# A four-stage token tower on one Trainium2 core: second-half attention operands on GpSimd and ScalarE, a norm split in two, routed input on 64-row tiles

## The chip, the cores and the metric

The kernel runs on one core of one Trainium2 chip, in one launch for the whole problem. The metric is the time of an execution on the device in microseconds (us). Three executions before the change gave a median of 1512.79 us (1504.69 to 1515.6). A further execution was profiled; its trace is the source of all rows.

## The reference, cut to what matters

```python
h = tok(x)                                        # masked scores, values, PReLU
h = layernorm(h + mamba(h))                       # 16-state scan
h = layernorm(h + experts(h))                     # 16 experts, top 2
h = layernorm(h + window_attention(h))            # this stage and its norm are touched
h = layernorm(h + routed_ffn(h))                  # its first matmul is touched

def window_attention(x):                          # windows of 64 tokens, 8 heads of 8
    q, k, v = split_heads(x @ w_qkv.T)            # x: 8 x 1024 x 64, float32
    a = q @ k.T * 8 ** -0.5 + rel_bias[rel_idx]
    return (softmax(a) @ v) @ w_proj.T + b_proj

def routed_ffn(x):
    h = relu(x @ Wi.T + bi)                       # 64 -> 128
    for l in range(2):
        h = relu(h @ (Ws[l] + Wr[l, route] + I).T + bs[l] + br[l, route])
    return h @ Wo.T + bo
```

## The kernel before

The eight sequences are worked on in four pairs, one after the other. A pair puts the 64 features of one sequence on partitions 0 to 63 and those of the other on 64 to 127; 1024 tokens lie along the free dimension, in two halves of 512 (`NC = 2`). All engines run written-out programs, and the order on each engine is the order in which the Python code emits its instructions; they meet at semaphores whose counts per pair stand in `PER`. There is no scheduler.

The attention runs in `NM = 8` steps of two windows. The operands come first: for each half, `att_inputs(c)` on TensorE makes keys, queries and values in PSUM (L687, L688, L691); ScalarE copies the keys (L985), scales the first head's block into `kb` (L987) and copies the queries (L990). `kb` holds the keys four times, each masked to one head. The other three heads are scaled by VectorE in `k_blocks(c)` (L1259). The values go to `vb`, four copies for each half: the first half on ScalarE (L999), the second on VectorE (L1283).

A step m then goes through: scores on TensorE (L735, `att_scores`), bias added and row maxima taken on VectorE (L1268, L1272, `bias_max`), maxima subtracted on GpSimd (L462, the shift), exponential on ScalarE (L1008), eight transposes on TensorE (L748, `att_turn`), their copy on ScalarE (L1014), products with the values on TensorE (L762, `att_values`), reciprocal and scaling on VectorE (L1296, L1301, `att_norm`), a transpose of the output (L768) with its copy on ScalarE (L1020), and the projection (L775), which adds to the residual in PSUM banks 6 and 7. TensorE's loop emits in turn s the scores of step s, the transposes of s-2, the value products of s-3, the output transpose of s-4 and the projection of s-5. Steps 0 to 3 belong to the first half, 4 to 7 to the second. In turn 1 it also puts the residual into banks 6 and 7 (L788).

A norm works on four chunks of 256 tokens (`NN = 4`): squares on ScalarE (L862), variance by a matmul with an averaging matrix (L486), Ln and Exp on ScalarE (L868, L873), product on VectorE (L1064 here, L1067 in the norm before). The norm of the attention, number 2, comes when all eight projections are done: ScalarE waits for `proj_ps` of all. Then the routed stage starts with `f_in`, L804: for each half, two matmuls over all 128 partitions with a weight `fiT` whose other half is zero, so that each picks one sequence; the routed layers follow at L814. The row maxima of step m must have been shifted before step m+2 overwrites the biased scores, and the shift's buffer is freed by the exponential two steps earlier.

## Time and profile before

| | before |
|---|---|
| median of three runs | 1512.79 us |
| these runs | 1504.69 to 1515.6 us |
| the profiled execution | 1513.76 us |
| its span, first to last instruction | 1512.0 us |
| TensorE matmul, VectorE, ScalarE, GpSimd busy | 85%, 68%, 39%, 30% |
| mean granted TensorE clock | 0.943 |

Times in the rows are microseconds from the first instruction unless marked ns. PE is TensorE's matmul, PEld its weight load, DVE is VectorE, ACT ScalarE, POOL GpSimd; L862 is line 862 of the kernel before. A granted clock of 1.00 is 2.4 GHz, 0.50 is 1.2 GHz. One float32 matmul of the program appears as two instructions in the trace. The third pair, whose attention runs from 1071 to 1117 us, is used for single rows.

### The profile page before, as it was taken

Reading aid. Unit: us, or ns where it says so; the run is one execution under the profiler, and the core shown is the slowest. Engines: PE = TensorE matmul, PEld = TensorE weight load, DVE = VectorE, ACT = ScalarE, POOL = GpSimd, SP = SyncE. Lnnn points to the kernel's source line nnn. Section 1 sums busy time; section 2 is a strip of 40 time slices with the busy share of each in tenths; the row PEclk is TensorE's granted clock in tenths of the full one; section 3 lists DMA queues with packets and bytes.
Section 4 is the critical chain, followed back from the end, with each engine's and each line's share of the span. In section 5 each row is a group of like instructions: output and inputs, shape, how many; then the busy total and the mean of one; then the engine's idle time right before and its main releaser. Section 6 shows DMA issues by size and latency. Waiting matters only on the chain. (4 is left out here: it accounts for less than half of the span.)

```text
span 1512.0 us, 16650 instructions
## 1 busy us (share of the span) xinstructions
PE 1292.1 (85%) x5930; PEld 562.1 (37%) x5930; DVE 1031.3 (68%) x1130; ACT 592.0 (39%) x815; POOL 455.7 (30%) x230
## 2 busy tenths in 40 slices
PE   6957789989995778998998677999899677899988
PEld 2222333348532223333742223333473232333366
DVE  3599965664449996567555999556756599865683
ACT  0354343333425344332525443532451634343245
POOL 3268800022005881001200788000210189600030
PEclk9979999997897999999999799999999889999998
DMA  8334420000003342000001344200000134220000
GB/s 245 104 129 155 146 69 12 1 1 1 15 0 129 143 143 83 22 1 1 2 15 44 113 149 143 69 2 1 1 1 15 59 125 167 98 57 0 1 2 15
DMA packets 43379, 93.66 MB, mean 62 GB/s; under 512 B 6786, under 2 KB 23970, under 8 KB 42786
## 3 DMA queue, kind: packets, MB, share of 16 engines
q1 hardware_dynamic: 42690, 88.25, 17.5%
q10 hardware_dynamic: 608, 4.34, 1.0%
q8 instruction: 49, 0.80, 0.2%
q14 instruction: 32, 0.26, 0.1%
HBM read 87.84 MB, written 4.73 MB: 61 GB/s over the span
## 5 line engine op out<-in xcount | busy, mean ns | idle before, releaser
L448 POOL TENSOR_TENSOR scratch<-scratch 128x1024 f32<-128x1024 f32 x124 | 297.4, 2413 | 354.7 <-DVE scratch L1152 353.1
L598 PE MATMUL ps<-scratch,consts 128*128 128x512 f32 x512 | 257.8, 638 | 6.2 <-POOL scratch L448 6.2
L462 POOL TENSOR_TENSOR scratch<-scratch,rmax 128x1024 f32<-128x1024 f32 x32 | 61.6, 1925 | 598.3 <-DVE rmax L1272 598.3
L1152 DVE TENSOR_TENSOR_SCAN scratch<-ps,scratch 128x1024 f32<-128x1024 f32 x100 | 225.5, 2278 | 0.5
L925 ACT ACTIVATE ps<-steps,vec 128x1024 f32<-128x1024 f32 x128 | 142.9, 1117 | 207.1 <-DVE scratch L1152 205.2
L1201 DVE TENSOR_TENSOR scratch<-scratch,ps 128x1024 f32<-128x1024 f32 x108 | 131.8, 1221 | 128.6 <-PE ps L659 117.7
L576 PE MATMUL ps<-bc,pick 128*128 128x512 bf16 x256 | 84.7, 416 | 139.0 <-DVE scratch L1141 101.7
L971 ACT ACTIVATE scratch<-ps 128x1024 f32<-128x1024 f32 x108 | 108.9, 1023 | 175.5 <-PE ps L646 175.5
L598 PEld LDWEIGHTS ps<-scratch,consts 128*128 128x128 f32 x512 | 104.8, 207 | 127.2 <-issue 100.5
L646 PE MATMUL ps<-h_odd,w 64*128 64x512 f32 x512 | 140.9, 636 | 3.8 <-ACT scratch L971 3.8
L1141 DVE TENSOR_TENSOR scratch<-steps,ps 128x1024 f32<-128x1024 f32 x100 | 122.0, 1220 | 28.8 <-PE ps L576 23.5
L659 PE MATMUL ps<-scratch,w 64*128 64x512 f32 x512 | 134.9, 602 | 7.2 <-DVE scratch L1201 7.2
L667 PE MATMUL ps<-scratch,to_model 128*64 128x512 f32 x512 | 138.1, 618 | 1.4 <-DVE scratch L1201 1.4
L1101 DVE TENSOR_TENSOR scratch<-ps,decayT 128x1024 f32<-128x1024 f32 x64 | 77.0, 1222 | 38.3 <-PE ps L515 26.5
L576 PEld LDWEIGHTS ps<-bc,pick 128*128 128x128 bf16 x256 | 19.0, 98 | 224.3 <-issue 218.0
L1208 DVE TENSOR_TENSOR scratch<-h_odd,ps 128x512 f32<-128x512 f32 x128 | 87.6, 687 | 19.3 <-PE ps L678 19.3
L456 POOL TENSOR_TENSOR work<-steps,work 128x1024 f32<-128x1024 f32 x28 | 66.1, 2360 | 33.2 <-ACT work L935 32.9
L659 PEld LDWEIGHTS ps<-scratch,w 64*128 64x128 f32 x512 | 47.3, 186 | 73.2 <-issue 70.7
L529 PE MATMUL ps<-scratch,xc 128*64 128x512 f32 x256 | 67.3, 614 | 4.5 <-DVE scratch L1101 4.5
L646 PEld LDWEIGHTS ps<-h_odd,w 64*128 64x128 f32 x512 | 39.7, 184 | 83.1 <-issue 83.1
L515 PE MATMUL ps<-steps 64*128 64x512 f32 x256 | 70.1, 634 | 0.0
L762 PE MATMUL ps<-vb,zs 128*128 128x36 f32 x512 | 65.6, 288 | 0.3
(197 smaller groups left out, 1610.0 us busy)
## 6 DMA issues: line engine op xcount, KB each, us to landing
scratch<-c_rows SPq DMA_DIRECT2D x128, 512.0 KB, 3.7
steps<-routed_table SPq DMA_DIRECT2D x128, 64.5 KB, 1.9
decayT<-in_decayT SPq DMA_DIRECT2D x8, 512.0 KB, 15.6
work<-in_table ACTq DMA_DIRECT2D x1, 2064.0 KB, 13.2
routed_table<-work SPq DMA_DIRECT2D x1, 2064.0 KB, 6.3
w<-in_w ACTq DMA_DIRECT2D x4, 512.0 KB, 20.8
out<-h_even SPq DMA_DIRECT2D x4, 512.0 KB, 2.6
bc<-in_x_next SPq DMA_DIRECT2D x3, 512.0 KB, 3.6
```

The costliest lines, as they stand in the source:

```text
L448: pool.tensor_tensor(hc_slot(k), hs_slot(k), c_slot(k), ALU.mult).then_inc(sem["hc_ready"], 1)
L576: m = mm(ps[:, c, :], pick[:, n:n + 1].to_broadcast([P, P]), bc[:, g, c * CH:(c + 1) * CH], start=True, stop=True)
L598: m = mm(ps[:, 6 + c, :], ident, hc_slot(k)[:, c * CH:(c + 1) * CH], start=(n == 0), stop=(n == NS - 1))
L646: m = mm(ps[:, first_bank(j) + g, :], w12[half, 0, e, :], h[1][half, c * CH:(c + 1) * CH], start=True, stop=True)
L659: m = mm(ps[:, 2 + g, :], w12[half, 1, e, :], x_gated(j)[half], start=True, stop=True)
L667: m = mm(ps[D * g:D * g + D, 4 + c, :], w3[:, e, :], hidden_slot(j)[:, g, :], start=False, stop=True, skip_group_check=True)
L925: act.activation(banks(dA_bank(k)), dt[:, k // NS, :], ACT.Exp, scale=v("A", k % NS))\
L971: act.activation(silu_slot(j), ps[:, first_bank(j):first_bank(j) + 2, :], ACT.Silu).then_inc(sem["silu_ready"], 1)
L1141: dve.tensor_tensor(dbu_slot(k), u[:, k // NS, :], banks(0), ALU.mult)\
L1152: dve.tensor_tensor_scan(hs_slot(k), banks(dA_bank(k)), dbu_slot(k), 0.0, ALU.mult, ALU.add).then_inc(sem["scanned"], 1)
L1201: dve.tensor_tensor(hidden_slot(j), silu_slot(j), ps[:, 2:4, :], ALU.mult).then_inc(sem["hidden"], 1)
L1208: dve.tensor_tensor(x_gated(j), h[1][:, c * CH:(c + 1) * CH], ps[:, 6 + j % 2, :], ALU.mult).then_inc(sem["x_gated"], 1)
```

## The change

Four edits, all in the attention and what follows it.

- The second half's three key blocks move from VectorE to GpSimd, behind the shift of step 1, with a semaphore of their own, `k_blocks_pool`, on which TensorE waits before the scores of the second half.
- The second half's four value copies move from VectorE to ScalarE, behind its `att_inputs(1)`.
- Chunks 0 and 1 of the attention's norm no longer wait for all projections. Their squares stand on ScalarE in turn 8, their variance matmuls on TensorE at the end of turn 9, their Ln and Exp on ScalarE in turn 9, ahead of the last copy of a transposed output. Chunks 2 and 3 follow the last projection; on TensorE their variance matmuls stand behind the first half's `f_in`. Their PSUM banks change.
- `f_in` uses the two 64-row halves of TensorE: `fiT` holds the weight once on each half, and each matmul reads 64 partitions. One memset at the start is dropped.

```diff
+                    if m == 1:
+                        pool.wait_ge(sem["k_copied"], at(pair, "k_copied", NC))
+                        for hh in range(K_SPLIT, HQ):
+                            pool.tensor_scalar(kb[:, WIN[1], hh, :],
+                                               k_sb[:, TOK[1]].rearrange("p (a b) -> p a b", b=WS),
+                                               head_mask[:, hh:hh + 1], None, ALU.mult)\
+                                .then_inc(sem["k_blocks_pool"], 1)
...
-        VAR_BANKS = ((2, 3, 4, 5), (0, 1, 6, 7), (0, 1, 2, 3), (6, 7, 2, 3))
+        VAR_BANKS = ((2, 3, 4, 5), (0, 1, 6, 7), (0, 1, 4, 5), (6, 7, 2, 3))
...
-                    pe.wait_ge(sem["k_blocks_dve"], at(pair, "k_blocks_dve", (HQ - K_SPLIT) * (c + 1)))
+                    pe.wait_ge(sem["k_blocks_dve"], at(pair, "k_blocks_dve", HQ - K_SPLIT))
+                    if c:
+                        pe.wait_ge(sem["k_blocks_pool"], at(pair, "k_blocks_pool", HQ - K_SPLIT))
...
                         att_proj(s - 5)
-                norm(2)
+                    if s == NM + 1:
+                        pe.wait_ge(sem["biased"], at(pair, "biased", NM))
+                        norm(2, range(NN // NC))
                 for c in range(NC):
                     pe.wait_ge(sem["h_ready"], at(pair, "h_ready", 2 * NN + NN // NC * (c + 1)))
                     for g in range(2):
-                        mm(ps[:, 2 * g + c, :], fiT[:, g, :], h[3][:, c * CH:(c + 1) * CH],
+                        half = slice(D * g, D * g + D)
+                        mm(ps[:, 2 * g + c, :], fiT[half, :], h[3][half, c * CH:(c + 1) * CH],
                            start=True, stop=True).then_inc(sem["f_in_ps"], 1)
+                    if c == 0:
+                        norm(2, range(NN // NC, NN))
...
                 att_inputs(1)
+                v_blocks(1)
                 for s in range(NM + 4):
...
+                    if s == NM:
+                        squares(2, range(NN // NC))
+                    if s == NM + 1:
+                        roots(2, range(NN // NC))
-                norm(2)
+                norm(2, range(NN // NC, NN))
...
                 bias_max(0)
-                k_blocks(1)
-                dve.wait_ge(sem["av_ps"], at(pair, "av_ps", NC))
-                av = ps[:, 5, :].rearrange("p (w g hp d) -> p w g hp d", w=NW // NC, g=2, hp=H // 2)
-                for a in range(2):
-                    half = slice(D * a, D * a + D)
-                    for g in range(2):
-                        dve.tensor_copy(vb[half, WIN[1], :, g, a, 0:HD], av[half, :, g, :, :])\
-                           .then_inc(sem["v_blocks_dve"], 1)
...
-            pool.memset(projT, 0.0)
-            pool.memset(fiT[:, :, :], 0.0).then_inc(zeroed, 1)
+            pool.memset(projT, 0.0).then_inc(zeroed, 1)
```

`norm` on ScalarE is now `squares` followed by `roots`, and `v_blocks(c)` is the old copy loop for either half. Line numbers shift: L1268, L1272 and L1296 become L1296, L1300 and L1316; L1008, L1014 and L1020 become L1032, L1038 and L1044; L486, L748, L762, L768, L775, L804, L814 become L493, L757, L770, L776, L783, L815, L827; L862, L868, L873 become L876, L885, L890.

VectorE at the start of the attention, before the change, from the maxima of step 0 to those of step 2:

```order
L1272 TENSOR_REDUCE rmax<-scratch 128x16 [waits biased]
L1259 TENSOR_SCALAR scratch<-scratch,consts 128x8x64 [waits k_copied]
L1259 TENSOR_SCALAR scratch<-scratch,consts 128x8x64 x2
L1283 COPY vb<-ps 64x32x8 [waits av_ps]
L1283 COPY vb<-ps 64x32x8 x3
L1268 TENSOR_TENSOR scratch<-ps,rows 128x1024 [waits att_ps]
L1272 TENSOR_REDUCE rmax<-scratch 128x16 [waits biased]
L1268 TENSOR_TENSOR scratch<-ps,rows 128x1024 [waits shifted,att_ps]
L1272 TENSOR_REDUCE rmax<-scratch 128x16 [waits biased]
```

The same place after it:

```order
L1300 TENSOR_REDUCE rmax<-scratch 128x16 [waits biased]
L1296 TENSOR_TENSOR scratch<-ps,rows 128x1024 [waits att_ps]
L1300 TENSOR_REDUCE rmax<-scratch 128x16 [waits biased]
L1296 TENSOR_TENSOR scratch<-ps,rows 128x1024 [waits shifted,att_ps]
L1300 TENSOR_REDUCE rmax<-scratch 128x16 [waits biased]
```

The three scalings (of `scratch`, where `kb` lies) and the four copies are gone; the bias of step 1 follows the maxima of step 0 directly.

TensorE at the end of the attention, before the change, from the output transpose of step 6 to the routed input:

```order
L762 MATMUL ps<-vb,zs 128x2x18 x7
L768 MATMUL ps<-consts,scratch 128x128 [waits normed]
L775 MATMUL ps<-scratch,to_model 64x64 [waits outT_sb]
L775 MATMUL ps<-scratch,to_model 64x64 x3
L768 MATMUL ps<-consts,scratch 128x128 [waits normed]
L775 MATMUL ps<-scratch,to_model 64x64 [waits outT_sb]
L775 MATMUL ps<-scratch,to_model 64x64 x3
L775 MATMUL ps<-scratch,to_model 64x64 [waits outT_sb]
L775 MATMUL ps<-scratch,to_model 64x64 x3
L486 MATMUL ps<-work,consts 128x256 [waits squared] x4
L804 MATMUL ps<-h_odd,fiT 128x512 [waits h_ready]
L804 MATMUL ps<-h_odd,fiT 128x512
```

After it, two places of the same program, the early variance matmuls and the end:

```order
L783 MATMUL ps<-scratch,to_model 64x64 x3
L493 MATMUL ps<-work,consts 128x256 [waits squared,biased]
L493 MATMUL ps<-work,consts 128x256 [waits squared]
L770 MATMUL ps<-vb,zs 128x2x18 [waits outT_sb,v_blocks,probT_sb]
L770 MATMUL ps<-vb,zs 128x2x18 x7
L776 MATMUL ps<-consts,scratch 128x128 [waits normed]
```

```order
L783 MATMUL ps<-scratch,to_model 64x64 x3
L815 MATMUL ps<-h_odd,fiT 128x512 [waits h_ready]
L815 MATMUL ps<-h_odd,fiT 128x512
L493 MATMUL ps<-work,consts 128x256 [waits squared] x2
L815 MATMUL ps<-h_odd,fiT 128x512 [waits h_ready]
L815 MATMUL ps<-h_odd,fiT 128x512
```

Two variance matmuls now stand ahead of the value products of step 7, the other two between the halves of the routed input.

ScalarE at the same end, after the change:

```order
L1038 ACTIVATE zs<-ps 128x1024 [waits pv_ps,probT_ps]
L1044 ACTIVATE scratch<-ps 128x128 [waits proj_ps,outT_ps]
L876 ACTIVATE work<-ps,out_bias 128x256 [waits proj_ps] x2
L1044 ACTIVATE scratch<-ps 128x128 [waits proj_ps,outT_ps]
L885 ACTIVATE work<-ps,vec 128x256 [waits var_ps] x2
L890 ACTIVATE work<-work 128x256 [waits act_chain] x2
L1044 ACTIVATE scratch<-ps 128x128 [waits proj_ps,outT_ps]
L876 ACTIVATE work<-ps,out_bias 128x256 [waits proj_ps] x2
```

Two squares stand between the output copies (L1044) of steps 5 and 6, two Ln and two Exp between those of steps 6 and 7; before, three such copies followed each other and all four squares came after them.

## Rows read from the trace of the kernel before

**Rows 1.** Busy time by window, attention to routed layers, first and third pair.
```profile
core 0: us, PE busy (x) PEld busy (x) DVE busy (x) ACT busy (x) POOL busy (x), PEclk, DMA share, GB/s
320.21:387.99 67.78, 60.99 (x449) 45.56 (x449) 35.78 (x62) 27.20 (x45) 15.39 (x8) 0.75 0.00 1
...
1070.89:1125.44 54.55, 47.87 (x449) 36.05 (x449) 35.78 (x62) 26.86 (x45) 15.40 (x8) 0.94 0.00 1
```

**Rows 2.** Timeline, third pair: start, length, engine, line, idle before and releaser.
```profile
1073.73 1.22 DVE L1272 TENSOR_REDUCE rmax<-scratch 128x16 f32<-128x1024 f32 x1
...
1074.86 2.92 DVE L1259 TENSOR_SCALAR scratch<-scratch,consts 128x512 f32<-128x512 f32 x3
...
1076.63 1.99 PE L788 MATMUL ps<-h_even,consts 128*128 128x512 f32 x4
...
1077.13 1.06 ACT L1008 ACTIVATE xc<-scratch 128x1024 f32<-128x1024 f32 x1 [1.69 <-POOL scratch L462]
...
1077.70 1.54 DVE L1283 COPY vb<-ps 64x256 f32<-64x256 f32 x4
1079.27 1.23 DVE L1268 TENSOR_TENSOR scratch<-ps,rows 128x1024 f32<-128x1024 f32 x1
...
1080.64 1.09 PE L735 MATMUL ps<-scratch 32*64 32x256 f32 x16 [2.02 <-DVE scratch L1268]
...
1081.83 1.90 POOL L462 TENSOR_TENSOR scratch<-scratch,rmax 128x1024 f32<-128x1024 f32 x1 [4.73 <-DVE rmax L1272]
...
1085.88 1.06 PE L748 MATMUL ps<-consts,xc 128*128 128x128 f32 x8 [1.62 <-ACT zs L1014]
...
1087.25 1.00 ACT L1014 ACTIVATE zs<-ps 128x1024 f32<-128x1024 f32 x1
...
1089.60 1.09 PE L748 MATMUL ps<-consts,xc 128*128 128x128 f32 x8
```

**Rows 3.** Busy time by window, third pair's middle steps and its end.
```profile
1090.00:1108.00 18.00, 18.00 (x196) 15.78 (x194) 14.02 (x24) 9.37 (x13) 7.61 (x4) 1.00 0.00 1
1114.00:1120.00 6.00, 5.06 (x34) 3.77 (x34) 1.09 (x4) 2.90 (x8) 0.00 (x0) 0.50 0.00 1
```

**Rows 4.** Timeline, third pair, from the last value products to the routed layers.
```profile
1112.16 2.06 PE L762 MATMUL ps<-vb,zs 128*128 128x36 f32 x16
...
1115.88 1.13 PE L775 MATMUL ps<-scratch,to_model 128*64 128x64 f32 x16
...
1117.06 1.57 ACT L862 ACTIVATE work<-ps,out_bias 128x256 f32<-128x256 f32 x4 [0.79 <-PE ps L775]
...
1117.59 3.51 PE L486 MATMUL ps<-work,consts 128*128 128x256 f32 x8 [0.57 <-ACT work L862]
...
1121.90 3.70 PE L804 MATMUL ps<-h_odd,fiT 128*128 128x512 f32 x8 [0.81 <-DVE h_odd L1064]
...
1125.44 7.31 PE L814 MATMUL ps<-scratch,steps 128*128 128x128 f32 x64
```

**Rows 5.** GpSimd's groups of instructions: busy us, mean ns | idle before.
```profile
L399 POOL MEMSET vb<- 128x2304 f32 x1 | 2.0, 2023 | 0.0
...
L415 POOL TENSOR_TENSOR in_x<-in_x,scratch 128x512 f32<-128x512 f32 x1 | 1.3, 1272 | 12.7 <-DMA route<-in_route 12.7
```

**Rows 6.** Timeline, third pair: half of the norm ahead of the attention.
```profile
1069.39 0.66 ACT L862 ACTIVATE work<-ps 128x256 f32<-128x256 f32 x2 [4.73 <-PE ps L667]
...
1069.83 1.13 PE L486 MATMUL ps<-work,consts 128*128 128x256 f32 x4 [0.48 <-ACT work L862]
1070.56 0.91 ACT L868 ACTIVATE work<-ps,vec 128x256 f32<-128x256 f32 x2 [0.51 <-PE ps L486]
...
1071.37 0.71 ACT L873 ACTIVATE work<-work 128x256 f32<-128x256 f32 x2
1071.81 0.76 DVE L1067 TENSOR_TENSOR h_even<-ps,work 128x256 f32<-128x256 f32 x2 [2.41 <-ACT work L873]
```

**Rows 7.** Chain of waits, expert stage: start us, us, what.
```profile
1343.16 1.06 PE ps L646 x4
```

More of the change, by code:

```diff
@@ L81 @@
     aq_ps=NC, ak_ps=NC, av_ps=NC, k_copied=NC, q_scaled=NC, k_blocks=NC * K_SPLIT,
-    k_blocks_dve=NC * (HQ - K_SPLIT), v_blocks=4, v_blocks_dve=4, att_ps=NM, biased=NM, row_max=NM, shifted=NM, att_exp=NM,
+    k_blocks_dve=HQ - K_SPLIT, k_blocks_pool=HQ - K_SPLIT, v_blocks=4 * NC, att_ps=NM, biased=NM, row_max=NM, shifted=NM, att_exp=NM,
     probT_ps=NM, probT_sb=NM, pv_ps=NM, normed=NW, outT_ps=NM, outT_sb=NM, proj_ps=NM,
@@ L144, in build_tower @@
         av_bd = sb("av_bd", [P, P])
-        fiT = sb("fiT", [P, 2, HID])
+        fiT = sb("fiT", [P, HID])
         c_dram = nc.dram_tensor("c_rows", (2, NS, T), F32, kind="Internal").ap()
@@ L342, in _ @@
                 (pick[:, :], i["pick"]), (out_wT, i["out_wT"]), (w3, i["w3"]),
-                (foT, i["foT"]), (fiT[0:D, 0, :], i["fiT"]), (fiT[D:P, 1, :], i["fiT"]),
+                (foT, i["foT"]), (fiT[0:D, :], i["fiT"]), (fiT[D:P, :], i["fiT"]),
                 (gate_bd[0:D, 0:NX], i["gate_w"]), (gate_bd[D:P, NX:2 * NX], i["gate_w"]),
@@ L753, in att_values @@
                     pe.wait_ge(sem["probT_sb"], at(pair, "probT_sb", m_ + 1))
-                    pe.wait_ge(sem["v_blocks"], at(pair, "v_blocks", 4))
-                    pe.wait_ge(sem["v_blocks_dve"], at(pair, "v_blocks_dve", 4))
+                    pe.wait_ge(sem["v_blocks"], at(pair, "v_blocks", 4 * NC if m_ else 4))
                     if m_ >= 2:
@@ L851, in then, with squares, roots @@
                     link(act, act_chain, per, pair, count, ins)
-                def norm(k, chunks=range(NN)):
+                def squares(k, chunks):
                     for c in chunks:
+                        part = c // (NN // NC)
                         if k == 1:
-                            act.wait_ge(sem["expert_ps"], at(pair, "expert_ps", NX * (c // (NN // NC) + 1)))
+                            act.wait_ge(sem["expert_ps"], at(pair, "expert_ps", NX * (part + 1)))
                         elif k == 2:
-                            act.wait_ge(sem["proj_ps"], at(pair, "proj_ps", NM))
+                            act.wait_ge(sem["proj_ps"], at(pair, "proj_ps", NM // NC * (part + 1)))
                         else:
-                            act.wait_ge(sem["r_ready"], at(pair, "r_ready", R_COUNT[k] + c // (NN // NC) + 1))
+                            act.wait_ge(sem["r_ready"], at(pair, "r_ready", R_COUNT[k] + part + 1))
                         act.activation(sq[:, c * NCH:(c + 1) * NCH], res_chunk(k, c), ACT.Square,
                                        bias=res_bias(k) if k >= 2 else 0.0).then_inc(sem["squared"], 1)
+                def roots(k, chunks):
                     before = count[0]
@@ L874, in norm @@
                     count[0] += len(chunks)
+                def norm(k, chunks=range(NN)):
+                    squares(k, chunks)
+                    roots(k, chunks)
                 for c in range(NC):
@@ L991, in att_inputs, with v_blocks @@
                        .then_inc(sem["q_scaled"], 1)
-                att_inputs(0)
-                act.wait_ge(sem["av_ps"], at(pair, "av_ps", 1))
-                av = ps[:, 4, :].rearrange("p (w g hp d) -> p w g hp d", w=NW // NC, g=2, hp=H // 2)
-                for a in range(2):
-                    half = slice(D * a, D * a + D)
-                    for g in range(2):
-                        act.activation(vb[half, WIN[0], :, g, a, 0:HD], av[half, :, g, :, :], ACT.Copy)\
-                           .then_inc(sem["v_blocks"], 1)
+                def v_blocks(c):
+                    act.wait_ge(sem["av_ps"], at(pair, "av_ps", c + 1))
+                    av = ps[:, 4 + c, :].rearrange("p (w g hp d) -> p w g hp d", w=NW // NC, g=2, hp=H // 2)
+                    for a in range(2):
+                        half = slice(D * a, D * a + D)
+                        for g in range(2):
+                            act.activation(vb[half, WIN[c], :, g, a, 0:HD], av[half, :, g, :, :], ACT.Copy)\
+                               .then_inc(sem["v_blocks"], 1)
+                att_inputs(0)
+                v_blocks(0)
                 norm(1, range(NN // NC, NN))
                 att_inputs(1)
+                v_blocks(1)
                 for s in range(NM + 4):
@@ L1276, in _ @@
                 bias_max(0)
-                k_blocks(1)
-                dve.wait_ge(sem["av_ps"], at(pair, "av_ps", NC))
-                av = ps[:, 5, :].rearrange("p (w g hp d) -> p w g hp d", w=NW // NC, g=2, hp=H // 2)
-                for a in range(2):
-                    half = slice(D * a, D * a + D)
-                    for g in range(2):
-                        dve.tensor_copy(vb[half, WIN[1], :, g, a, 0:HD], av[half, :, g, :, :])\
-                           .then_inc(sem["v_blocks_dve"], 1)
                 def att_norm(m_):
```

## The prediction

> **What bounds the kernel now.** I read the page's busy shares first: TensorE carries 85% of the span, VectorE 68%, but the shares mix stages with different limits, so the edited stretch has to be read by itself. The table of windows gives it for two of the four pairs, from the first scores of the attention to the first routed matmul [rows 1]. In the third pair it takes 54.55 us with TensorE busy for 47.87, in the first 67.78 us, with the same instructions at a mean granted clock of 0.75 instead of 0.94. All four together are 231 us of the 1512, and everything outside them is left as it was but for one memset.
>
> The timeline of the third pair then tells what ends last in it. Read [rows 2] from the top: VectorE finishes the row maxima of step 0, spends 2.92 us on the key blocks of the second half and 1.54 us on its value blocks, and only then adds the bias of step 1, at 1079.27. Its scores had been there since 1076.63, when TensorE went on to the next line. TensorE waits 2.02 us for that addition, and 1.62 us more two steps later. From 1090 to 1108 it is busy for 18.00 of 18.00 us [rows 3]: there TensorE alone sets the pace, and what is won before is carried along. Behind the last projection comes a serial chain at the clock's lower level (1114 to 1120: 0.50, so 1.2 GHz) [rows 3, 4]: four squares, four variance matmuls, four Ln and Exp, four products, then the routed input, 8.4 us from the first square at 1117.06 to the first routed matmul at 1125.44 [rows 4].
>
> **The head.** All arithmetic is for the third pair. Without the 2.92 and 1.54 us the bias of step 1 can start when its scores are there, 1076.75 with a hop, instead of 1079.27. But TensorE still has the four matmuls that end at 1078.62 in front of the scores of step 2, which began at 1080.64: the head can give at most 2.0 us [rows 2].
>
> The three key blocks now stand on GpSimd between the shift of step 1 and that of step 2. Queued behind them are the shifts; ScalarE's exponential waits for the shift, its copy of the transposed probabilities stands behind the exponential, and TensorE's next transposes wait for that copy. The bias takes 1.23 and the maxima 1.22, so shift 1 runs from 1079.3 to 1081.25; with a price p for a block, shift 2 ends at 1083.15 + 3p, the exponential (1.06) and the copy (1.00) at 1085.2 + 3p, and the transposes of step 2 start at 1085.35 + 3p where they started at 1089.60 [rows 2]. So the head gives 4.25 - 3p, no more than 2.0.
>
> No row shows p. Below stands the rate of the GpSimd memset of 2304 columns, 2.02 us, which is 0.45 us for 512 columns with nothing read; above, the 512-column GpSimd product of two tensors, 1.27 us [rows 5]. The nearest row is the shift itself: one full tensor, 16 repeated values, 1.90 us for 1024 columns, so 0.95 for 512 [rows 2]. A block reads one tensor and a single column, a little less: I take **p = 0.9, gain 4.25 - 2.7 = 1.55 us** (2.0 at the lower end, 0.43 at the upper).
> The Trainium skill (GPSIMD Engine Reference, sections 3.1 and 4.1) calls GpSimd the wrong engine for ordinary elementwise work, yet nearly line rate with one input; its best measured case for 512 elements, 0.77 us, taken as an estimate of p, would make the head 1.94. Its warning speaks against the move, and the 1.55 to 1.94 us between the two values of the head's arithmetic show how little turns on it.
> At p = 0.9 the blocks are ready at 1083.95. The scores of step 4, their first reader, stand on TensorE behind the transposes of step 1 (at 1085.88 before, at 1083.9 at the earliest now [rows 2]) and the value products of step 0, so they find them ready.
>
> The value blocks on ScalarE cost nothing: four copies took VectorE 1.54 us, and ScalarE sits idle 1.69 us in front of the exponential of step 0 [rows 2]. Without that cover the exponential would end 1.5 us later, at 1079.7; its transposes stand behind scores that start at 1078.6 at the earliest and take 1.1, so even that would be hidden.
>
> **The tail.** Three things move. First, half of the norm leaves the chain. At full clock a half norm, two squares to the end of two products, took 1069.39 to 1072.57, 3.2 us [rows 6]. Behind the last projection there now run: this half (3.3 with the longer form of its last operation), with the first half's routed input between squares and matmuls. On two row tiles of 64 that input costs what a pair of 64-row matmuls costs in the expert stage, 1.06 us [rows 7], against 3.54 / 2 = 1.77 for half of the old form [rows 4]. It begins with the squares while the variance matmuls could have begun 0.44 later, so it adds 0.6; the second half's input adds 1.06. Sum 3.3 + 0.6 + 1.06 = 5.0 instead of 8.4: 3.4 us won. ScalarE and VectorE read these results as before.
>
> Second, the early half stands in front of other work. On TensorE two variance matmuls (1.13 us [rows 6]) and a wait for the squares, some 0.3, stand ahead of the value products of step 7: 1.4 us. What is queued behind: these products, the last reciprocals, the last transposes, the last projections, so the whole end of the chain. On ScalarE the two Ln and two Exp (0.91 + 0.71 less a little overlap, 1.5 us [rows 6]) stand ahead of the last copy of the output's transpose; between the copies of steps 6 and 7 there is most of that room, and I let 0.3 stick out (0 to 1.5). So 3.4 - 1.7 = 1.7 us at the clock of before.
>
> Third, the clock. The old stretch ran at 0.50; its eight variance instructions took 3.51 us, four at full clock 1.13 [rows 4, 6]. With the new matmuls in between the clock may stay up, which is worth 0.5 more (2.2), or fall later, over both halves of the routed input and the last variances: 2 x 1.06 + 0.6 lost, -1.0. I take **1.2 us**, since the stretch is still thin on TensorE.
>
> **The sum.** (1.55 + 1.2) x 4 = 11.0. The smaller memset of the routed weight frees the loads behind it 0.3 us sooner, once; the loads are the same in number. 1513.76 (span and start-up of the profiled execution) - 11.3 = 1502.5. The median of the runs shown is 1.0 below that execution, so the forecast for a median is **1501.5 us**. Both ends of both prices give 4 x (0.43 - 1.0) = -2.3 to 4 x (2.0 + 2.2) = 16.8 us, 1515 to 1496.
>
> **The rivals.**
> *The first pair loses its slow stretch.* It took 13.2 us more than the third with the same instructions, all of it at the lower clock [rows 1]. What went before was thin work on TensorE, with waits like the 2.02 and 1.62 us of [rows 2], and the change takes the first of them away. Against it: the three other pairs have the same waits and kept their clock, so a small shift decides. 1501.5 - 13.2 = 1488.
>
> *One more pair falls into it.* Each pair now starts its attention at another moment than before, and the wait of the second transposes for the copy stays. 1501.5 + 13.2 = 1515.
>
> *The change moves the wait only.* Blocks at 1.27 us hold the shifts, and the early norm half costs TensorE what it saves: (0.43 + 0) x 4 = 1.7, 1511. For it speaks that TensorE runs without a gap from 1090 on [rows 3], so that 1.4 us put into its order there are paid in full.
>
> *Slower.* The place is the same, the transposes of step 1 with TensorE waiting; the price is 13.2 us a pair; it decides from the second additional pair on: 1501.5 + 26.4 = 1528, with a third 1541. Against it: only one pair of four showed it.
>
> **How the numbers follow.** Forecast, 1496 to 1507: 0.42. First pair clean, about 1488: 0.22. One more slow pair, about 1515: 0.15. Wait only moved, 1507 to 1515: 0.13. Two more slow pairs: 0.08. The range 1488 to 1517 leaves out half of the clean case and the last one, some 0.2. The line between faster and same is 1% of 1512.79, so 1497.7, and 1527.9 on the other side, about what a measurement of this kernel can tell from no change. Faster: the clean case and the best of the forecast, 0.22 + 0.09 = 0.31; slower 0.08; same 0.61. The likeliest outcome by itself is thus a small gain of 0.7% (1496 to 1507).
>
> **What the profile of the changed kernel would show.** VectorE's bias of step 1 starts about 1.8 us after the maxima of step 0 end, where it was 4.3. Three GpSimd scalings of 0.9 us between the second and third shift. TensorE's wait of 2.02 us gone, the second transposes' wait still there. Two variance matmuls ahead of the last value products, four instructions of 64 rows in about 1.06 us for each half of the routed input, and some 5 us from the last projection to the first routed matmul. The stretch in pairs two to four at about 51.8 us instead of 54.5. I am wrong if a scaling takes over 1.4 us, if the stretch's mean clock falls below 0.9 in more than one pair, or if the roots hold the last copy by more than 1 us.

## The result and the profile after

The changed kernel takes 1534.03 us in the median of four runs (1531.84 to 1538.66), the kernel before 1514.19 beside it. The ratio is **1.0123 [1.0067, 1.0179]**: slower by 1.2%, where 1501.5 with a range of 1488 to 1517 was forecast. A second group of runs on another occasion gave 1533.77 and 1.0105 [1.0027, 1.0182]. The kernel before spreads from 1502 to 1533 us by itself, of which more below. Ratios compare fast executions alone and so leave out those of a kernel that are over 1.5% above its fastest; beside the experiments these were 13 of 25, 8 of 19 and 4 of 13 executions of the kernel before, and its medians with them are 1527, 1523 and 1516 us.

The windows of the changed kernel, from the first scores to the first routed matmul of the four pairs (columns: window, its length, busy time and count of TensorE, its weight loads, VectorE, ScalarE, GpSimd, then the granted clock, the DMA share and GB/s):

```profile
325.23:385.40 60.17, 52.05 (x450) 39.73 (x449) 31.33 (x55) 27.30 (x48) 19.77 (x11) 0.86 0.00 1
700.50:760.66 60.16, 52.04 (x449) 39.72 (x448) 31.33 (x55) 27.31 (x48) 19.77 (x11) 0.86 0.00 1
1076.31:1136.46 60.15, 52.03 (x450) 39.71 (x449) 31.33 (x55) 27.30 (x48) 19.77 (x11) 0.86 0.01 1
1451.56:1511.71 60.15, 52.03 (x449) 39.71 (x448) 31.33 (x55) 27.41 (x48) 19.77 (x11) 0.86 0.00 1
1094.00:1111.00 17.00, 15.71 (x92) 12.94 (x93) 6.62 (x13) 6.59 (x9) 4.81 (x3) 0.54 0.01 2
```

All four pairs are alike, at 60.15 us with a clock of 0.86. Before, the third took 54.55 and the first 67.78 [rows 1]. So three pairs lost 5.5 to 5.7 us each and the first won 7.6. Of the 18.0 us between the two spans (1512.0 and 1530.0) the pairs two to four hold 16.8, the first -7.6, its later beginning 5.0 (325.23 against 320.21, where the second profile of the kernel before starts at 326.39, so this does not go with the change), and the rest, between and behind the stretches, 3.8.

The timeline of the third pair shows where the 5.6 come from (start, length, engine, line, what, and in brackets the idle time ahead of it):

```profile
1082.19 1.22 DVE L1296 TENSOR_TENSOR scratch<-ps,rows 128x1024 f32<-128x1024 f32 x1 [1.82 <-PE ps L744]
...
1083.97 1.09 PE L744 MATMUL ps<-scratch 32*64 32x256 f32 x16
...
1084.75 1.90 POOL L461 TENSOR_TENSOR scratch<-scratch,rmax 128x1024 f32<-128x1024 f32 x1 [2.40 <-DVE rmax L1300]
...
1086.63 4.65 POOL L470 TENSOR_SCALAR scratch<-scratch,consts 128x512 f32<-128x512 f32 x3
...
1091.24 3.76 POOL L461 TENSOR_TENSOR scratch<-scratch,rmax 128x1024 f32<-128x1024 f32 x2
1091.64 1.09 PE L744 MATMUL ps<-scratch 32*64 32x256 f32 x16
...
1093.18 1.06 ACT L1032 ACTIVATE xc<-scratch 128x1024 f32<-128x1024 f32 x1 [4.39 <-POOL scratch L461]
...
1094.14 1.01 ACT L1038 ACTIVATE zs<-ps 128x1024 f32<-128x1024 f32 x1
...
1095.29 1.94 PE L757 MATMUL ps<-consts,xc 128*128 128x128 f32 x8 [2.56 <-ACT zs L1038]
...
1097.02 3.25 PE L770 MATMUL ps<-vb,zs 128*128 128x36 f32 x15
```

VectorE is free at once, as intended: the bias of step 1 comes 1.82 us after the maxima of step 0 and the scores of step 2 no longer wait. But three GpSimd blocks take 4.65 us, and behind them stand shift 2, its exponential, the copy, and TensorE, idle for 2.56 us ahead of the transposes of step 2. From there its clock is 0.50: eight transposes take 1.94 us instead of 1.09, and the low stretch lasts 17 us in every pair (the last row of the windows is the third's). The end of the stretch:

```profile
1130.50 0.94 PE L783 MATMUL ps<-scratch,to_model 128*64 128x64 f32 x16
...
1131.43 1.13 PE L815 MATMUL ps<-h_odd,fiT 64*128 64x512 f32 x4
...
1132.49 1.13 PE L493 MATMUL ps<-work,consts 128*128 128x256 f32 x4
...
1134.47 0.88 DVE L1092 SCALAR_TENSOR_TENSOR h_odd<-ps,out_bias,work 128x256 f32<-128x256 f32 x2 [3.09 <-ACT work L890]
...
1135.40 1.13 PE L815 MATMUL ps<-h_odd,fiT 64*128 64x512 f32 x4 [1.78 <-DVE h_odd L1092]
...
1136.46 7.41 PE L827 MATMUL ps<-scratch,steps 128*128 128x128 f32 x64
```

From the end of the last projections, 1131.44, to the first routed matmul it takes 5.02 us, at full clock, where it took 8.43 [rows 4] with a clock of 0.50 up to about 1120.7 and of 1.00 behind that. So the tail does what it was to do, and the loss lies between the transposes of step 2 and the last projections. In a table, in us, with two experiments from below:

| third pair | first scores to transposes of step 2 | to the end of the last projections | to the first routed matmul | sum |
|---|---|---|---|---|
| before | 18.71 | 27.41 | 8.43 | 54.55 |
| changed | 18.98 | 36.15 | 5.02 | 60.15 |
| changed, TensorE kept busy (e6) | 20.03 | 28.15 | 5.01 | 53.19 |
| changed, blocks on ScalarE (e4) | 16.35 | 28.21 | 5.02 | 49.58 |

### The profile page after: what moved, and what is told of

Read it like the earlier page. It is cut to its first block and busy times, and to the rows that moved or that the text cites. A ratio compares the mean times of both kernels' runs of the same rounds, so it can differ in the third digit from the quotient of the medians.

```text
span 1530.0 us, 16613 instructions
## 1 busy us (share of the span) xinstructions
PE 1294.0 (85%) x5914; PEld 568.2 (37%) x5930; DVE 1019.2 (67%) x1102; ACT 596.5 (39%) x831; POOL 474.2 (31%) x241
## 5 line engine op out<-in xcount | busy, mean ns | idle before, releaser
L605 PE MATMUL ps<-scratch,consts 128*128 128x512 f32 x512 | 254.7, 631 | 6.3 <-POOL scratch L447 6.3
L770 PEld LDWEIGHTS ps<-vb,zs 128*128 128x128 f32 x512 | 74.5, 230 | 0.2
L770 PE MATMUL ps<-vb,zs 128*128 128x36 f32 x512 | 73.3, 307 | 0.0
```

Source lines behind the costliest of these rows:

```text
L605: m = mm(ps[:, 6 + c, :], ident, hc_slot(k)[:, c * CH:(c + 1) * CH], start=(n == 0), stop=(n == NS - 1))
L770: last = mm(o[:, :, hp, :], att_probT(m_)[:, b * P:(b + 1) * P], vb[:, 2 * m_ + ww, hp].rearrange("p g a b -> p g (a b)"), start=True, sto ...
```

## The experiments

The theory: GpSimd's blocks hold shift 2, TensorE idles, its clock falls for 17 us, and this costs 8 us a pair. The rivals: the new tail costs the time; the low clock is chance; the late shift costs by itself, whatever the clock. Times are medians of up to ten executions; pairs are read from the one that was profiled, which for e1, e2, e4, e5, e6 and e9 took 5 to 13 us less than the median. What the longer executions held is not shown.

**One edit undone, and each half of the change alone.** e1 puts the three key blocks back on VectorE:

```diff
-                    if m == 1:
-                        pool.wait_ge(sem["k_copied"], at(pair, "k_copied", NC))
-                        for hh in range(K_SPLIT, HQ):
-                            pool.tensor_scalar(kb[:, WIN[1], hh, :],
...
                 bias_max(0)
+                k_blocks(1)
...
```

> The changed kernel with one edit undone: the three key blocks of the second half stand on VectorE again, behind the row maxima of step 0; the values on ScalarE and the early norm half stay. Theory (the GpSimd blocks of 1.57 us hold the shift of step 2, TensorE waits 2.56 us for its transposes, and its clock falls to 0.50 for 17 us in every pair): the 2.56 us wait and the 0.50 stretch at the transposes of step 2 are gone in at least three pairs, the stretch from first scores to first routed matmul is 50 to 52 us there instead of 60.15, and the time is 1495 to 1508. Rival (the early norm half, or chance, brings the low clock): the low stretches stay in three or four pairs, 1525 to 1540.

Measured: 1523.7 us, ratio to the kernel before 1.0071 [1.0009, 1.0133]; the profiled execution took 1510.78. The time missed the expectation by 16 us. Of the mechanism, half came: the wait ahead of the transposes of step 2 is gone in all four pairs, but only two took 50.49 us at full clock, where at least three were expected; the others took 60.04 and 53.54.

```profile
325.77:376.26 50.49, 44.08 (x449) 33.29 (x448) 34.07 (x58) 27.31 (x48) 15.39 (x8) 1.00 0.00 1
691.95:751.99 60.04, 53.62 (x450) 40.74 (x449) 34.07 (x58) 27.41 (x48) 15.39 (x8) 0.83 0.00 1
```

Here TensorE waits 1.76 us ahead of the transposes of step 1 in every pair (VectorE's 2.92 us of blocks are late there), and with that wait one pair of four fell to 0.50 for 20.5 us, another for 3.4. So with the GpSimd blocks every pair falls, and without them fewer do, but they are not the only way to it.

e2 is the head of the change alone, on the kernel before (the same blocks on GpSimd, the same values on ScalarE, nothing of the norm):

```diff
+                    if m == 1:
+                        pool.wait_ge(sem["k_copied"], at(pair, "k_copied", NC))
+                        for hh in range(K_SPLIT, HQ):
+                            pool.tensor_scalar(kb[:, WIN[1], hh, :],
...
-                k_blocks(1)
...
+                v_blocks(1)
...
```

> The kernel before with the head of the change alone: key blocks of the second half on GpSimd behind the shift of step 1, their values on ScalarE; norm and routed input as before. Theory: the wait of about 2.56 us ahead of the transposes of step 2 and 17 us of 0.50 clock in all four pairs, the stretch about 62.8 us in each (60.15 and the 2.6 that the tail gave), so some 8 us more in three pairs and 5 less in the first: 1530 to 1545. Rival (the tail costs the time, the head is worth about nothing): 1510 to 1516, clock stretches as in the kernel before.

Measured: 1548.21 us, 3 above the interval, 1.0263 [1.0172, 1.0353]. Three pairs took 64.75 to 64.84 us at 0.79, the last 57.88. The first and the last:

```profile
323.25:388.00 64.75, 57.70 (x449) 42.84 (x449) 31.51 (x55) 28.44 (x49) 19.77 (x11) 0.79 0.00 1
1462.18:1520.06 57.88, 50.84 (x449) 38.13 (x449) 31.51 (x55) 28.55 (x49) 19.77 (x11) 0.88 0.01 1
```

TensorE waits 2.56 us ahead of the transposes of step 2 in all four, and the clock falls behind it in all four, in the last for only 7 us. The head alone costs more than the whole change, so the tail is not the cause.

e3 is the tail alone, on the kernel before (early norm half, 64-row routed input):

```diff
+                    if s == NM + 1:
+                        pe.wait_ge(sem["biased"], at(pair, "biased", NM))
+                        norm(2, range(NN // NC))
...
-                        mm(ps[:, 2 * g + c, :], fiT[:, g, :], h[3][:, c * CH:(c + 1) * CH],
+                        half = slice(D * g, D * g + D)
+                        mm(ps[:, 2 * g + c, :], fiT[half, :], h[3][half, c * CH:(c + 1) * CH],
...
```

> The kernel before with the tail of the change alone: norm's first half inside the last steps and the routed input on 64-row tiles; key and value blocks as before. Theory: the tail gives 2.6 us a pair and leaves the clock in the head as it was: 1499 to 1506, stretch 52 us in pairs with the full clock. Rival (the tail's new order brings the low clock or costs as much as it saves): 1513 or more.

Measured: 1515.9 us, 1.0026 [0.9981, 1.0072]: neither the gain nor the loss. The expected gain did not come, and the time is the one that its rival had named (1513 or more). The four windows:

```profile
322.93:376.36 53.43, 45.57 (x450) 33.98 (x449) 35.59 (x62) 25.84 (x44) 15.40 (x8) 0.97 0.00 1
691.82:754.93 63.11, 55.26 (x450) 42.36 (x449) 35.58 (x62) 26.05 (x44) 15.39 (x8) 0.81 0.01 1
1070.59:1125.56 54.97, 47.10 (x449) 34.39 (x448) 35.59 (x62) 25.89 (x44) 15.40 (x8) 0.92 0.00 1
1445.09:1500.23 55.14, 47.28 (x450) 35.86 (x449) 35.59 (x62) 25.95 (x44) 15.39 (x8) 0.94 0.01 1
```

With the old head the pairs keep its waits of 2.02 and 1.62 us, and in the second and the fourth the clock falls behind them, as in the first pair before. In the first and the third it falls only at the end: from the last projections to the first routed matmul it takes 6.26 and 7.80 us there, against 5.02 in the changed kernel. The tail's own gain is only whole where the clock holds; part of it can also be given back a little later, which is told with e4.

**Another place for the blocks.** e4 puts them on ScalarE behind the exponential of step 0, where it idled 3.08 us in the changed kernel:

```diff
-                    if m == 1:
...
                         act.activation(att_prob(s), att_shift(s), ACT.Exp).then_inc(sem["att_exp"], 1)
+                        if s == 0:
+                            act.wait_ge(sem["k_copied"], at(pair, "k_copied", NC))
+                            for hh in range(K_SPLIT, HQ):
+                                act.activation(kb[:, WIN[1], hh, :],
+                                               k_sb[:, TOK[1]].rearrange("p (a b) -> p a b", b=WS),
+                                               ACT.Copy, scale=head_mask[:, hh:hh + 1])\
...
```

> The changed kernel with the three key blocks of the second half on ScalarE behind the exponential of step 0 (about 0.6 us each, in the 3.1 us that it idles there) in place of GpSimd. Theory: neither VectorE nor GpSimd is held, the wait of 2.56 us goes and the clock stays up at the transposes of step 2 in at least three pairs: stretch 49.5 to 51.5 us there, 1490 to 1505, at or below the version with the blocks on VectorE. Rival (the low clock comes by chance or from the tail): 1520 or more, whatever engine has the blocks. Second rival (the wait alone costs, its clock nothing): 1.5 to 2.5 us a pair, 1524 to 1530.

Measured: 1496.66 us, **0.9893 [0.9836, 0.9950]**. Three blocks take 1.93 us there, and in the profiled execution (1489.43 us) all four pairs hold the full clock:

```profile
1054.21:1103.79 49.58, 44.01 (x450) 33.20 (x449) 31.33 (x55) 29.14 (x51) 15.22 (x8) 1.00 0.01 2
1103.80:1107.20 3.40, 3.40 (x19) 3.40 (x18) 0.75 (x1) 1.83 (x5) 0.00 (x0) 0.54 0.00 0
```

The second window is the 3.4 us behind the first routed matmul: the clock is low there instead of ahead of it, and the 64 routed matmuls take 9.04 us, 1.6 longer than the 7.41 of the third pair of the changed kernel. So it is in three of e4's four pairs; in the fourth they take 7.41. From the first routed matmul to the next pair's first scores it takes 315.66, 315.67 and 315.93 us behind these three, and 314.31, 313.95 and 313.95 in the kernel before. So of the 2.6 us that the tail wins inside the stretch about 1.7 are given back behind it where the clock falls there.

e5 leaves the blocks on GpSimd, but one behind each of the shifts 0, 1 and 2:

```diff
-                    if m == 1:
+                    if m < HQ - K_SPLIT:
...
+                        hh = K_SPLIT + m
...
```

> The changed kernel with its three GpSimd key blocks apart: one behind each of the shifts of steps 0, 1 and 2, where GpSimd idled 2.4 us, instead of all three behind the shift of step 1. Theory (4.65 us in one place hold shift 2 too long): the first block hides, the second delays shift 2 by about 0.6 us and the third shift 3 by as much; TensorE's wait for the transposes of step 2 shrinks from 2.56 to under 1 us and the clock stays up in most pairs: stretch 49.6 to 51 us there, 1490 to 1508. Rival (GpSimd is the wrong place for these blocks wherever they stand): low clock in three or four pairs, 1520 or more.

Measured: 1502.93 us, 0.9931 [0.9882, 0.9979] (one of its ten executions took 1546.59), stretch 49.80 to 49.85 us with clock 1.00 in all four pairs. The third:

```profile
1054.92:1104.77 49.85, 44.07 (x450) 33.28 (x449) 31.33 (x55) 27.18 (x48) 19.77 (x11) 1.00 0.01 2
```

Each block still takes 1.56 us; GpSimd as such is not the fault, 4.65 us in one place are.

**The wait or the clock.** e6 keeps the changed kernel and its late shift, and gives TensorE products of zeros to add to a residual bank while it waits:

```diff
...
+                    if s == 2 + 2:
+                        for k in range(16):
+                            mm(ps[:, 6, 0:P], zeros[:, :], ident, start=False, stop=True,
+                               skip_group_check=True)
                     if 0 <= s - 2 < NM:
                         att_turn(s - 2)
```

> The changed kernel with the blocks where it has them, but TensorE is given something to do in its wait: sixteen products of zeros, 128x128 each, added to a bank of the residual (about 2.2 us) ahead of the transposes of step 2, so that it idles there for a few tenths of a microsecond only. Theory A (the idle time brings the clock down, and the low clock is what costs): the transposes of step 2 start as late as before (about 19 us after the first scores), yet no 17 us stretch of 0.50 follows; the stretch is 52 to 53 us instead of 60.15 and the time 1497 to 1510. Theory B (the late shift costs by itself, or the clock falls for another reason than this idle time): stretch 60 us as in the changed kernel, 1525 to 1540.

Measured: 1513.92 us, 0.9972 [0.9920, 1.0023], 4 us above the interval of theory A and 11 below that of B. The timeline of the third pair:

```profile
1078.11 3.84 PE L801 MATMUL ps<-consts,zeros 128*128 128x128 f32 x32
...
1081.78 1.04 PE L759 MATMUL ps<-consts,xc 128*128 128x128 f32 x8
```

and the window of the same pair:

```profile
1061.75:1114.94 53.19, 47.64 (x481) 36.84 (x481) 31.32 (x55) 27.17 (x48) 19.76 (x11) 1.00 0.01 2
```

The sixteen products took 3.84 us instead of the 2.2 I had worked out, so the transposes of step 2 even start 1.05 us later than in the changed kernel (20.03 against 18.98). Still the stretch is 7.0 us shorter, because the clock stays up in all four pairs. This parts the loss: against e4 the late transposes cost 3.6 us a pair (53.19 - 49.58), the low clock 7.0 more (60.15 - 53.19). Since the products themselves made the transposes 1.05 us later, the wait's share is too large by that in this reckoning; by the table, changed kernel against e4, it is 2.6 us ahead of the transposes of step 2 (18.98 - 16.35) and 7.9 behind them (36.15 - 28.21).

e8 goes the other way: it takes e4 and holds shift 2 with a GpSimd memset that is longer in each pair:

```diff
+                    if m == 1:
+                        pool.memset(spare[:, 0:3100 + 900 * pair], 0.0)
...
```

> The version with the blocks on ScalarE, and behind the shift of step 1 one GpSimd memset of a spare tile, longer in each pair: 3100, 4000, 4900 and 5800 columns, by 0.88 us per 1000 columns 2.7, 3.5, 4.3 and 5.1 us (the three blocks took 4.65). Theory (any work of this length there holds shift 2, and TensorE's clock falls with its wait): the transposes of step 2 start about 0.7, 1.5, 2.3 and 3.1 us later than the 16.35 us of the version without it; the first pair keeps its full clock, the last one falls to 0.50 for some 17 us and its stretch is about 8 us longer than its wait explains; the two between show where it turns. Rival (the low clock has to do with the blocks or their writes, not with the wait): no pair falls, each is longer by its delay alone, 50.3 to 52.7 us.

Measured: 1508.84 us. TensorE's transposes of step 2, one row of the timeline a pair:

```profile
342.89 1.06 PE L752 MATMUL ps<-consts,xc 128*128 128x128 f32 x8 [0.55 <-ACT zs L1040]
...
708.91 1.06 PE L752 MATMUL ps<-consts,xc 128*128 128x128 f32 x8 [1.30 <-ACT zs L1040]
...
1074.63 1.06 PE L752 MATMUL ps<-consts,xc 128*128 128x128 f32 x8 [2.05 <-ACT zs L1040]
...
1447.54 1.86 PE L752 MATMUL ps<-consts,xc 128*128 128x128 f32 x8 [2.80 <-ACT zs L1040]
```

and the windows of its four pairs:

```profile
325.91:376.08 50.17, 44.05 (x450) 33.20 (x449) 31.33 (x55) 29.03 (x51) 17.75 (x9) 1.00 0.00 1
691.19:742.10 50.91, 44.05 (x449) 33.20 (x448) 31.33 (x55) 29.14 (x51) 18.50 (x9) 1.00 0.01 2
1056.15:1112.63 56.48, 48.87 (x449) 36.19 (x448) 31.33 (x55) 29.19 (x51) 19.25 (x9) 0.91 0.01 1
1428.32:1488.71 60.39, 52.03 (x449) 39.72 (x449) 31.33 (x55) 29.13 (x51) 20.00 (x9) 0.86 0.00 1
```

Waits of 0.55 and 1.30 us cost about what they are long (50.17 and 50.91 against 49.58). At 2.05 and 2.80 the clock falls too and the pair is 6.9 and 10.8 us longer. The blocks and their writes have nothing to do with it: a memset of a tile that nobody reads does the same. Hold and number of the pair go together in this run; but in the changed kernel and in e2 all eight pairs fell behind a wait of 2.56 us, and in e9 below none of four behind 0.92, so it is not the number.

**The price of a block.** e7 has six GpSimd forms behind the last shift, off the path:

```diff
+                    if m == NM - 1:
...
+                        pool.tensor_scalar(b(1), a, head_mask[:, 1:2], None, ALU.mult)
+                        pool.tensor_scalar(b(2), a, 0.5, 1.0, ALU.mult, ALU.mult)
+                        pool.tensor_tensor(b(3), a, head_mask[:, 1:2].to_broadcast([P, 512]), ALU.mult)
+                        pool.tensor_tensor(b(4), a, a, ALU.mult)
+                        pool.tensor_copy(b(5), a)
+                        pool.memset(b(6), 0.0)
```

> Price of GpSimd forms, off the path: the version with the blocks on ScalarE, and behind the last shift of each pair six GpSimd instructions on 128x512 in whole rows of a tile of their own: product with a column per partition, with two constants, with a repeated column as second tensor, of a tensor with itself, a copy, a memset. Theory (the instruction with one column per partition is itself slow): the first takes 1.5 to 1.6 us, as in the changed kernel. Rival (the scattered output, pieces of 32 columns, makes it slow): the first takes 0.9 or less, near a copy. The product of two tensors 1.27 and the memset 0.45 as in the kernel before. Time as the version it is built on, 1488 to 1505.

Measured (1489.8 us), the timeline of GpSimd in the third pair:

```profile
1086.64 1.57 POOL L472 TENSOR_SCALAR spare<-spare,consts 128x512 f32<-128x512 f32 x1
1088.18 0.62 POOL L473 TENSOR_SCALAR spare<-spare 128x512 f32<-128x512 f32 x1
1088.76 1.04 POOL L474 TENSOR_TENSOR spare<-spare,consts 128x512 f32<-128x512 f32 x1
1089.76 1.04 POOL L475 TENSOR_TENSOR spare<-spare 128x512 f32<-128x512 f32 x1
1090.74 0.61 POOL L476 COPY spare<-spare 128x512 f32<-128x512 f32 x1
1091.29 0.52 POOL L477 MEMSET spare<- 128x512 f32 x1
```

The product with one column per partition takes 1.57 us into whole rows as well, so the scattered output is not what costs. It is 2.5 times the same instruction with constants (0.62), and 1.5 times a product of two full tensors. e9 uses that: the changed kernel, its blocks where they are, but with the mask's column as a repeated second tensor:

```diff
-                            pool.tensor_scalar(kb[:, WIN[1], hh, :],
+                            pool.tensor_tensor(kb[:, WIN[1], hh, :],
                                                k_sb[:, TOK[1]].rearrange("p (a b) -> p a b", b=WS),
-                                               head_mask[:, hh:hh + 1], None, ALU.mult)\
+                                               head_mask[:, hh:hh + 1].unsqueeze(2).to_broadcast([P, NW // NC, WS]),
+                                               ALU.mult)
...
```

> The changed kernel, its GpSimd blocks in the same place, but written as a product of two tensors with the mask's column repeated, which took 1.04 us in the run on prices where the form with one column took 1.57. Theory (the price of the block decides): three take 3.1 us, the transposes of step 2 start 16.35 + 3.1 - 2.0 = 17.4 us after the first scores, a length at which the run with memsets kept its clock (17.72): stretch 50.5 to 50.8 us in all pairs, 1490 to 1508, 25 us under the changed kernel. Rival (GpSimd writing these blocks there is harmful at any price near one microsecond): stretch 55 to 60 us, 1515 or more.

Measured: 1509.84 us, 0.9964 [0.9915, 1.0013]. A block takes 1.04 us, TensorE waits 0.92 us ahead of the transposes of step 2, at 17.34 us, and no pair falls there (third pair):

```profile
1064.17:1115.26 51.09, 44.62 (x450) 33.22 (x449) 31.33 (x55) 27.29 (x48) 18.12 (x11) 0.99 0.01 2
```

The stretch is 0.3 us over the upper end of what was expected (51.08 to 51.15) and the median 2 us above the interval: the clock is low for the last 1.2 us of each stretch, and the stages between the stretches take 317.5 us here, against 315.7 in e4.

**The same kernels again.** The changed kernel on one chip with e4, and a second profile of the kernel before.

> The changed kernel itself, on the same chip as the other three runs of this group. Theory: all four pairs fall to 0.50 for 17 us again, stretch 60.2 us in each, 1530 to 1540, with little spread between its executions, since no pair is at the edge. Rival (the four low stretches were chance): two or fewer of them, 1510 to 1525.

Measured: 1533.77 us (1530.39 to 1534.26), 1.0105 [1.0027, 1.0182]; the pairs take 60.75, 60.13, 60.16 and 60.14 us. The four low stretches are not chance; only the first began sooner, behind the wait of 1.34 us ahead of the transposes of step 1.

> The kernel before, profiled once more, since its times here spread from 1503 to 1532. Theory (its head is at the edge: waits of 2.02 and 1.62 us after which a pair keeps its clock or not): the number of pairs with a low stretch of 17 to 24 us in the head explains the time, about 1503 with none, 1512 with one, 1523 with two, 1531 with three. Rival (the spread comes from the stages outside the attention): the heads as in the first profile, one low pair, at any time.

Measured: 1511.27 us, one low pair (the first, 57.66 us, low for 6.8 us in the head) and three at 54.68 to 54.69. That agrees with one fallen pair at 1512, though this fall was shorter than I had said; one profile can't settle what spreads the times of this kernel.

> The version with the blocks on ScalarE behind the exponential of step 0 once more, beside the changed kernel on one chip. Theory: stretch 49.6 us and full clock in all four pairs, 1488 to 1504, 2 to 3% under the changed kernel and 0.5 to 1.6% under the kernel before. Rival (its first result was chance): a low stretch in one pair or more, 1505 or above.

Measured: 1502.69 us, 0.9883 [0.9780, 0.9986], so the gain over both kernels is there again, 2.0% under the changed kernel by the medians (one of its four executions took 1517.19). But the profiled execution (1501.67) shows the rival's low stretch in the first of its windows:

```profile
324.92:385.67 60.75, 55.19 (x450) 42.30 (x449) 31.33 (x55) 29.22 (x51) 15.21 (x8) 0.80 0.00 1
701.32:750.89 49.57, 44.01 (x450) 33.21 (x449) 31.33 (x55) 29.11 (x51) 15.21 (x8) 1.00 0.01 2
```

and, of the timeline, the transposes of step 1 in the first and the third pair:

```profile
337.55 1.58 PE L749 MATMUL ps<-consts,xc 128*128 128x128 f32 x8 [1.34 <-ACT zs L1037]
...
1079.17 1.06 PE L749 MATMUL ps<-consts,xc 128*128 128x128 f32 x8 [1.34 <-ACT zs L1037]
```

The wait of 1.34 us ahead of the transposes of step 1 stands in both pairs; in the first the clock falls behind it, in the third it does not. Of the sixteen profiled pairs with this wait and none behind it in the head that is as long (e4, e5, e7, e12) one fell. It is 11.2 us, and the two profiled executions of this version lie 12.2 us apart.

## Why the prediction was wrong, step by step

**VectorE's relief: right.** Bias of step 1 at 1.82 us after the maxima (said: 1.8), the wait of 2.02 us gone, the values on ScalarE hidden, the blocks ready for the scores of step 4 (1091.28 against 1091.64, by much less than said).

**The price of a block: the first step that failed.** I took 0.9 us, between 0.45 and 1.27; it is 1.566. I had called the product of two full tensors the upper bound, since a block reads less. In the chip's forms that is no bound: e7 has the form with a column slower than two tensors. The arithmetic around it held: 4.25 - 3 x 1.566 = -0.45 us for the head, measured -0.27 (18.71 to 18.98 us from the first scores to the transposes of step 2). My own line, a scaling over 1.4 us, was crossed.
The Trainium skill (GPSIMD Engine Reference, section 4.1) calls work with one input roughly line-rate on GpSimd. The runs here agree for the copy and the constants (0.61 and 0.62 us for 512 columns), not for the operand of one column per partition (1.57).

**The sum: a wait was charged by its length, the second step that failed and the one that took the time out of the range.** With p = 1.566 my sum would have been (-0.45 + 1.2) x 4 + 0.3 = 3.3 us won, 1509.5, within the range. What it lacks is a term for the clock behind the wait that a late shift makes: the sum put it at nothing. From the transposes of step 2 to those of step 7 the third pair takes 27.14 us instead of 19.19, 8.0 us more with the same instructions, 24 us in pairs two to four. That 1509.5 + 24 comes so near to the 1534.03 measured is partly luck: between the two profiles the first pair won 7.6 us, and 8.8 were lost outside the four stretches. In the slower rival I had this mechanism, TensorE waiting and the clock falling at the transposes, with 0.08. Three things in it were off: the place (step 2, since shift 2 is what the blocks hold; I had step 1, where single pairs of either kernel did fall too), the price (8 us, not the 13.2 of the first pair), and above all the chance, which I took as independent of p. It was not: e8 has the same stretch with and without the fall by the length of the hold, and e9 repairs it with p = 1.04. The first pair [rows 1] had shown what such a wait can set off.

**The tail: about right.** 5.02 us from the last projections to the routed matmuls (said: 5.0). The early half makes the way to the end of the last projections 0.8 us longer (9.01 us from the transposes of step 7, 8.22 before), not 1.7; but the last of the 8.22 ran at the lower clock (the value products of step 7 took 2.06 us there, 1.87 now), so at one clock it costs more than 0.8, how much is not shown. The roots hold no copy. I had read the whole old chain as running at the lower clock; its last five microseconds did not. The tail is worth 2.6 us inside the stretch, above the 2.2 that I had as its upper end. Where the clock then falls at the routed matmuls (in one of the changed kernel's four pairs, in two of four when it was profiled again, in three of e4's) 1.6 are given back and 1.0 is left; I had taken 1.2 and named a later fall as the lower bound. The stages between the stretches also take 0.8 to 1.7 us longer in the changed kernel (315.10, 315.65 and 315.10 us against 314.31, 313.95 and 313.95); the routed matmuls explain the second of these, and what the other two come from is open.

**What stays open.** Which of the pairs with a wait of 1.3 to 2.0 us falls, and with it the spread of 10 to 30 us between executions of one kernel, these runs don't settle.

## What to carry to other kernels

Price a moved instruction in its exact form, operand kinds included: a row of another form, even of one that reads more, need not bound it. When work is moved in front of something that TensorE waits for, work out the length of its longest wait and put the clock's price beside it: here a wait of 2.56 us made a pair 9.1 us longer than one of 0.92 at the same place (60.15 and 51.09). And look for the idle time on the engine that is idle at that moment (ScalarE, 3.08 us), or spread the work over several gaps, before taking the engine that is idlest on average.

## What the runs showed of the hardware

- GpSimd on 128x512 float32: column per partition 1.57 us, two tensors 1.04 (the second repeated or not), constants 0.62, copy 0.61, memset 0.52; writing pieces of 32 columns instead of whole rows made no difference (1.566 both). The 1.27 us product before the change [rows 5] is of the same kind as the 1.04; why it was longer there was not tried.
- ScalarE does the same scaling by a column in 1.93 us for three in a row, 0.64 each (e4).
- TensorE's granted clock was at 0.50 (1.2 instead of 2.4 GHz) behind the waits of 2.05 to 2.80 us ahead of the transposes of step 2 in e8's two pairs, in e2's four and in seven of the changed kernel's eight (in the eighth it had fallen behind the wait of 1.34 before that); behind waits of 0.55 and 1.30 us (e8) and of 0.92 (e9, four pairs) at that place it was not. It stayed low for 6 to 17 us. Shorter waits ahead of the transposes of step 1 were followed by a fall in some pairs only: 1.34 us in two of the forty profiled pairs that had it, 1.76 us in two of four (e1), 2.02 and 1.62 us one behind the other in four of twelve (the kernel before twice, e3). With products of zeros in the wait it stayed up in four pairs of four (e6).
